# Attention probabilities times V: a delay of four tiles instead of six, issued ahead of the scores

## What is computed

```python
scores = jnp.einsum('bsqhd,bthd->bqhst', qh, kh) * scale
probs = jax.nn.softmax(scores, axis=-1)
a_dot = jnp.einsum('bqhst,bthd->bsqhd', probs, vh)
```

## Time and profile before

| | us |
|---|---|
| median of 2 timed runs | 3163.11 (3157.97 to 3168.24) |
| the profiled execution | 3157.07 |
| its span on the slowest core (core 3) | 3155.4 |
| spans of the 8 cores | 3127.2 to 3155.4 |
| busy on that core: PE, ACT, DVE, POOL | 2436.2, 963.2, 595.4, 590.9 |

### The profile page before, as it was taken

How to read it: one execution, slowest core, us unless ns; L and a number is a source line. 1 busy time by engine, 2 the same in 40 slices (tenths; PEclk the granted TensorE clock), 3 DMA queues, 4 the chain that set the end, 5 groups by cost and what they waited for, 6 DMA issues and landing times.

```text
span 3155.4 us, 40984 instructions; the slowest of 8 cores (3127.2 to 3155.4 us)
## 1 busy us (share of the span) xinstructions
PE 2436.2 (77%) x14265; PEld 1334.8 (42%) x14265; DVE 595.4 (19%) x1657; ACT 963.2 (31%) x1671; POOL 590.9 (19%) x1071
## 2 busy tenths in 40 slices
PE   3677666777744699968999777776449997799986
PEld 1223222222211487824778322221117775277752
DVE  2322332111136300020000011112460003010010
ACT  2200030988830122201222059886102221022210
POOL 1100010000000133323333310000003332333333
PEclk9788878888865799989999988887559998999999
DMA  4222214000000499979999960000009997999999
GB/s 115 74 41 47 42 65 120 3 4 4 3 2 1 145 360 355 361 272 370 359 347 362 357 233 4 4 4 3 0 1 340 360 354 250 396 335 361 356 339 350
DMA packets 161916, 591.77 MB, mean 188 GB/s; under 512 B 20920, under 2 KB 23096, under 8 KB 157368
## 3 DMA queue, kind: packets, MB, share of 16 engines
q0 software_dynamic: 151344, 552.14, 51.3%
q1 hardware_dynamic: 10376, 37.01, 3.6%
HBM read 325.23 MB, written 8.39 MB: 106 GB/s over the span
## 4 chain that ended last, share of the span: by engine, by line
PE 57%; DVE 12%; ACT 11%; DMA 11%; issue 8%; DVEq 1%; SPq 0%; POOL 0%; ACTq 0%; POOLq 0%
PE pAB L704 14%; PE pAB L695 14%; ACT arena L472 10%; DMA warena<-wd 8%; PE pCD L296 5%; PE pAB L296 4%; PE pCD L666 3%; PE pE L484 3%; PE pAB L452 3%; PE pF L484 2%; PE pAB L569 2%; PE pF L666 2%; PE pE L666 2%; PE pT L238 2%; DVE x L624 1%
## 5 line engine op out<-in xcount | busy, mean ns | idle before, releaser
L695 PE MATMUL pAB<-ln_fm,warena 128*128 128x256 bf16 x4096 | 492.5, 274 | 14.1 <-DMA warena<-wg 11.3
L704 PE MATMUL pAB<-ln_fm,warena 128*128 128x256 bf16 x4096 | 490.5, 273 | 8.7 <-DMA warena<-wu 6.6
L685 POOL DMA_DIRECT2D warena<-wg x256 | 136.3, 532 | 1752.7 <-PE pAB L695 1061.0
L695 PEld LDWEIGHTS pAB<-ln_fm,warena 128*128 128x128 bf16 x4096 | 398.7, 98 | 123.6 <-issue 38.3
L704 PEld LDWEIGHTS pAB<-ln_fm,warena 128*128 128x128 bf16 x4096 | 399.8, 98 | 61.4 <-issue 14.0
L472 ACT ACTIVATE arena<-pAB,bias_s 128x512 bf16<-128x512 f32 x512 | 369.7, 722 | 68.7 <-PE pCD L459 64.8
L472 ACT ACTIVATE arena<-pCD,bias_s 128x512 bf16<-128x512 f32 x512 | 372.2, 727 | 0.0
L452 PE MATMUL pAB<-q_fm,k_fm 64*128 64x512 bf16 x512 | 222.3, 444 | 164.5 <-ACT arena L472 157.6
L711 ACT ACTIVATE gtmp<-pAB,sg_s 128x256 bf16<-128x256 f32 x256 | 121.4, 474 | 563.1 <-PE pAB L704 504.4
L719 DVE TENSOR_TENSOR arena<-gtmp,utmp 128x256 bf16<-128x256 bf16 x256 | 75.0, 293 | 1057.5 <-ACT utmp L715 1057.5
L459 PE MATMUL pCD<-q_fm,k_fm 64*128 64x512 bf16 x512 | 227.9, 455 | 0.0
(11 more groups left out here) (118 smaller groups left out, 2073.6 us busy)
## 6 DMA issues: line engine op xcount, KB each, us to landing
warena<-wd POOLq DMA_DIRECT2D x512, 512.0 KB, 6.0
warena<-wg POOLq DMA_DIRECT2D x256, 512.0 KB, 3.7
warena<-wu POOLq DMA_DIRECT2D x256, 512.0 KB, 4.7
xstage<-x SPq DMA_DIRECT2D x16, 1024.0 KB, 5.6
warena<-wqt POOLq DMA_DIRECT2D x16, 512.0 KB, 5.9
x<-x SPq DMA_DIRECT2D x8, 1024.0 KB, 14.5
y<-x SPq DMA_DIRECT2D x8, 1024.0 KB, 5.4
warena<-wkt POOLq DMA_DIRECT2D x8, 512.0 KB, 5.9
```

The source lines that it names most:

```text
L695: ttg = P.do("t", lambda e, it=it, wb=wb, c=c: e.matmul(pA[0:128, 0:256], wgb[wb][:, c, :], ln2_fm[:, c, 0:256], start=(c == 0), stop=(c = ...
L704: ttu = P.do("t", lambda e, it=it, wb=wb, c=c: e.matmul(pB[0:128, 0:256], wub[wb][:, c, :], ln2_fm[:, c, 0:256], start=(c == 0), stop=(c = ...
```

## The change

In the loop over key tiles the delay of AV goes from six tiles to four, and AV is issued ahead of the scores of the same round instead of behind them. The loop has 20 rounds instead of 22.

```diff
-                for tc in range(22):
+                for tc in range(20):
+                    if tc >= 4:
+                        tca = tc - 4
+                        for st in range(2):
+                            j = prs[st]
+                            t_av[(j, tca)] = P.do(
+                                "t", lambda e, j=j, tca=tca, st=st:
+                                e.matmul(avbank[st][0:65, 0:512],
+                                         v_tm[:, tca, j % 8, 0:65],
+                                         A_et[:, st * 8 + tca % 8, :],
+                                         start=(tca == 0), stop=(tca == 15)),
+                                waits=[t_exp[(j, tca)],
+                                       war_av[st] if tca == 0 else None],
+                                inc=True)
                     if tc < 16:
...
-                    if tc >= 6:
-                        tca = tc - 6
-                        for st in range(2):
...
```

## The result

The changed kernel takes 3135.02 us in the median of 11 runs, and the kernel before 3167.67 in the median of 10. The ratio is 0.9887 with a 95% interval of 0.9866 to 0.9908, so 1.1% faster: 35.8 us of 3167.67, between 29 and 42. That is clear of no change, and within the 2% that I named as the bound. Runs in which one die of the chip held a lower clock are left out of the ratio but not out of the medians, which is why the medians are only 32.7 us apart.

The account below looks back on a forecast made before the run. The exponentials on ACT, with gaps, were taken to bound the attention stage. A shorter pair end (26.6 us) plus an earlier first AV (9.3) gave 35.9 us, so 3124 us from 3160, range 3107 to 3147.

Parts of the forecast that it names:

- Shorter end of a pair: End of each head pair: eight AV behind the last scores, ACT idle 0.98 us instead of 1.81; gain 26.6 us.
- Earlier first AV: Start of each head pair: 3.7 us without AV instead of 7.41, so fewer clock falls; gain 9.3 us.
- dearer: Rival, rounds after a clock fall: falls stay as frequent and cost more since rounds hold AV; 3146 us, chance 0.19.
- Steady rounds: Rounds within a head pair: nothing added, 1.157 us at the high clock level and 1.54 at the low.
- The copies: DVE copies ahead of a pair's first AV: 0.48 us left, costed at nothing; rival that they hold AV up 3134, chance 0.03.
- The clock stays up: Rival, start of each head pair: 3.7 us without AV too few for a fall; gain 50.0, 3110 us, chance 0.13.
- The low level persists: Rival, whole head pair: rounds take 1.54 us throughout, 4.57 us more each pair; 3306 us, chance 0.03.
- the swing between levels: Rule against the change, rounds with AV: brief PE idling swings the clock and loses throughput; result then a slower rival.

Follow-up runs that it names:

- late_first_short_end: Changed kernel with seven rounds of scores ahead of the first AV as before, still eight AV behind the last scores; pass 325.6 to 329.0 us, before 337.6.
- d6_ahead: Changed kernel with the delay kept at six tiles, AV still ahead of the scores; pass 326.3 to 329.0 us, against 337.6 before.
- d4_behind: Kernel before with the delay cut to four tiles, AV still behind the scores; pass 324.6 to 328.0 us, against 337.6 before.
- before_filled: Kernel before with two unused 128x512 matmuls behind the scores of tiles 1 to 5; pass 325.4 to 326.5 us, against 337.6 before.
- early_first_long_end: Changed kernel with 14 AV behind the last scores as before, rounds 7, 10 and 13 without AV; pass 326.1 to 328.5 us, before 337.6.
- d3_ahead: Changed kernel with a delay of three tiles; pass 316.9 to 319.9 us, ratio to the kernel before 0.9854.
- d2_ahead: Changed kernel with a delay of two tiles; pass 335.7 to 342.8 us, against 319.6 for the changed kernel.
- the filler matmuls: Changed kernel with two unused 128x512 matmuls behind the scores of tiles 1 to 3; ratios to the kernel before 0.9809 and 0.9829 in two runs.
- all runs of the table: The kernels compared by length of a pass and distance between head pairs, including the kernel before (337.6 us) and the changed kernel (319.6 us).

## Why the prediction was right

The forecast was a gain of 35.9 us and a time of 3124, on a base of 3160. The gain measured is 35.8 (29 to 42) by the ratio and 35.9 by the passes. That it is met to a tenth is chance, at an interval 13 us wide. The time of 3135.02 is 11 us over the forecast, inside the range of 3107 to 3147. That part is not the change: the kernel before came to 3167.67 and not to my base of 3160, and the medians differ by 32.7 where the ratio gives 35.8. The ratio applied to 3160 gives 3124.3.

*Shorter end of a pair.* Right, step by step: the last AV 0.14 us behind the last exponential (0.15 foreseen), then 0.31 and 0.51, and a bracket of 0.97 against 0.98. late_first_short_end shows that this term stands by itself (its idle time is 0.97 while the clock falls in every distance), and d6_ahead and d4_behind that it is used up at 10 AV.

*Earlier first AV.* The size was right, 0.31 us for each distance (0.74 to 0.43) where 0.29 was foreseen. That it is the clock was argued then, and before_filled shows it. The two numbers behind it were off in opposite directions. I took three falls in five; there were 10 to 13 in the 15 distances of a pass, 72%. I priced each at 0.73, and it is 0.43/0.72 = 0.60. To the first: I let the clock fall only in pairs where it would do so inside the 3.7 us without AV. Of the 172 falls in the changed kernel 100 come after the first AV of the pair has started, by up to 1.4 us. What PE does ahead of the thin rounds may have a part too, as early_first_long_end suggests. To the second: a stretch at the low level lasts about 4 us in the changed kernel and about 7 in the one before, so it is left sooner with AV in the rounds, as I had it against the rival "dearer". So the product came out right by some luck, and the rule "time without AV" is not the whole of it.

*Steady rounds.* They stayed at 1.157 us, and at 1.5 at the low level.

*The copies.* Costed at nothing, and no wait for them is seen: they end at 745.81, and the first AV starts at 746.74. They also start sooner than I had it. The first copy reads only head A, whose last AV does not wait for the last exponential, so it starts 0.10 us ahead of the last AV (742.76 and 742.86) and not 0.27 behind it. The margin is small all the same: AV waits for the copies twice on the slowest core of d3_ahead, and in nearly every pair of d2_ahead.

*The rivals.* "The clock stays up" did not come, but is what the filler matmuls make of it: 0.9829 against 0.9887. "The low level persists" did not come: no stretch at the low level in the changed kernel's attention lasts more than 7 us. Nor did the swing between levels that the Trainium skill describes (TensorE: Matmul & The Clock Gate, "A second HAM failure mode: psum-queue depth-cycling") come in steady rounds with AV: early_first_long_end and before_filled go through 200 us at a granted clock of 1.00 while PE idles a fifth of a microsecond in more than half of their rounds. In all runs of the table every fall comes 1.8 to 6.5 us after the last AV of a pair, so in the rounds without AV or in the first ones behind them, and there the trace agrees with it.

## What to carry to other kernels

Where a loop is software-pipelined anew for each outer step, the delay is paid twice: at the end as a queue of the delayed work ahead of the next step's first instruction, and at the start as rounds without it. Shorten the delay until the last delayed instruction waits for its input, but leave the time that the copies of the finished step need; here a delay of two tiles gave the gain back. Then issue the next step's first work ahead of that last instruction. Here the first gave 1.1%, and the second, together with the filler, about 1.4% more (0.9873 to 0.9734, the latter known to one per cent). Look at the granted clock of the thin rounds as well: here PE had too little to do in them and became the bound a few microseconds later, which cost 0.74 us of 21.17 in each pair, and work that nobody reads paid for itself.

## What was not expected

Extra matmuls made the kernel before faster: 160 more in each pass, and the pass is 12 us shorter (337.6 to 325.9). And an order that is bad at the end of a pair, 14 AV in a row, went with few falls of the clock: early_first_long_end had none in its first passes and 2 to 6 in its second, where the changed kernel, with the same four rounds of scores behind eight AV, had 10 or more in each. Why its two passes differ stays open.
